# Second cross attention: turned scores ahead of scores in each slot, and two kinds of copies on VectorE instead of ScalarE

## The chip, the cores and the metric

The kernel runs on one core of a Trainium2 chip. The metric is the device time of one execution in microseconds. The core's engines work through programs of their own, each in order, and wait for each other by semaphores: TensorE (matrix products, into PSUM), VectorE, ScalarE, GpSimd, and SyncE (SP, here only a queue that starts DMAs).

## The reference

The reference is a decoder of two layers over x [16, 256, 256], each with an attention, a cross attention and experts. The change is in the cross attention of the second layer:

```python
def _L1_xattn_ref(q, k, v, mask, Wq, Wk, Wv, Wo):
    DIM, HEADS = (256, 16)
    HD = DIM // HEADS
    qh = (q @ Wq).reshape(b, s, HEADS, HD).transpose(0, 2, 1, 3)
    kh = (k @ Wk).reshape(b, s, HEADS, HD).transpose(0, 2, 1, 3)
    vh = (v @ Wv).reshape(b, s, HEADS, HD).transpose(0, 2, 1, 3)
    g = jnp.einsum('bhqd,bhkd->bhqk', qh, kh) / jnp.sqrt(jnp.float32(HD))
    g = g - mask * 1000000000.0
    A = jax.nn.softmax(g, axis=-1)
    att = jnp.einsum('bhqk,bhkd->bhqd', A, vh)
    att = att.transpose(0, 2, 1, 3).reshape(b, s, DIM)
    return att @ Wo
x = x + _L1_xattn_ref(_layernorm(x, axis=-1), ctx_1024, ctx_1024, mask_Bx1x1xS2_fk0, ...)
```

There are 16 batches of 256 queries and 256 keys, and 16 heads of 16 values.

## The kernel before, in words

The stages of the decoder run one behind the other. `l1_cross_attend` (its tiles are called x1a) gets the projected q and k as rows of heads in DRAM and v in SBUF, and does scores, softmax, the product with v, and the output projection. Sixteen heads are eight pairs (`PAIRS`), and one batch is eight **slots** h, one for each pair. `HALF` is 4, `LAG` is 6, `TPB` is 2 (256 rows are two tiles of 128).

In a slot TensorE does three things:

- `scores(b, p, h)` (L2228): four products into one of two PSUM tiles `s_ps`, of pair h of batch b, rows are queries. They serve only to find each row's maximum. It waits until VectorE's maximum of two slots before has emptied the tile. VectorE's `maximum` (L2372) reduces them, one instruction of 128x1024 values a slot, and in slots 3 and 7 `split_top` (L2378) writes the negated maxima of four pairs as a high and a low part.
- `turned_scores(b, p, h - 6)` (L2240): the same scores once more with keys as rows, six slots later: four products and, added to each by a second product (L2252), the negated maximum, which is read from `mT`. They go to the one tile `st_ps`, so they wait until ScalarE's exponentials of the slot before have emptied it. In slots 0 to 5 they are pairs 2 to 7 of the batch before. ScalarE's `exponents` (L2313) is two instructions of 128x512.
- in odd slots the **pieces**, small steps that use two PSUM banks `fill` in turn, in the order of a list (L2171). Their names are letters: M turns the maxima (half 0 in slot 5, half 1 in slot 1), P is the product of probabilities and v for two pairs, B turns that product back, O turns the normalised result, W is the output projection. A piece waits until the piece before it in its bank has been drained, and W also for O's parts.

The list: slot 1: M1, B3, P0. Slot 3: B0, O, P1. Slot 5: M0, B1, W, P2. Slot 7: B2, P3. Banks alternate along it, so P0 uses M1's bank, P1 uses B0's, W uses M0's, P2 uses B1's.

Before the change the drains are split so: ScalarE copies M (to `mT`, L2330), P (to `oT`, L2334) and O (L2338, L2340); VectorE drains B by a reciprocal and a product into `out` (L2396, L2400), and W by an addition to the resident x, followed by the row statistics. In each slot ScalarE's program has the exponentials first and then the drains of the slot in the list's order; VectorE's has the maximum, the split in slots 3 and 7, and then its drains. GpSimd copies the mask and v of a batch and makes O's low part (L2365). SP loads the rows of heads two batches ahead once the turned scores of half a batch are done (L2219).

The loops are written out for batches 0 to 3, then go over batches 4 to 15 in pairs, and batches 16 and 17 hold what is left over from 14 and 15, without scores.

Of the kernel before, what the change touches and what calls it, by code (L numbers as in the profile page):

```python
# [14 lines left out]
P = 128  # L15
BATCH = 16
SEQ = 256
# [1225 lines left out]
class Plan:  # L1243
# [21 lines left out]
    def done(self, piece, b):  # L1265

        return self.counts[piece.kind] * (b + piece.ahead) + piece.number + 1
# [579 lines left out]
PAIRS = HEADS // 2  # L1847
# [4 lines left out]
def live(b):  # L1852

    return not isinstance(b, int) or 0 <= b < BATCH
# [280 lines left out]
def l1_cross_attend(nc, sh, head_rows, wo, v, sel, mask_col, qk, top_rows):  # L2135
# [4 lines left out]
    HALF = PAIRS // 2  # L2140
    QUADS = PAIRS // 2
    LAG = 6
    with ExitStack() as ctx:
# [34 lines left out]
        def pieces_of(h):  # L2178
            return [(i,) + piece[0:3] for i, piece in enumerate(order) if piece[3] == h]
# [15 lines left out]
        with nc.Block() as block:  # L2195
# [31 lines left out]
            def _(pe):  # L2227
                def scores(b, p, h, turn):  # L2228
                    if h % HALF == 0:
                        pe.wait_ge(s_ld[p][h // HALF], 16 * LOADS * (turn + 1))  # L2230
                    if not (isinstance(b, int) and b == 0 and h < 2):
                        pe.wait_ge(s_max, PAIRS * b + h - 1)
                    for t in range(TPB):
                        for n in range(2):
                            r = slice(64 * n, 64 * n + SCORE_ROWS)
                            last = pe.matmul(s_ps[h % 2][:, n, t * SEQ:(t + 1) * SEQ], qk[p][r, 0, h, t * P:(t + 1) * P],  # L2236
                                             qk[p][r, 1, h, :], start=True, stop=True)
                    last.then_inc(s_sc, 1)
# [51 lines left out]

                def batch(b, p, turn=None):
                    for h in range(PAIRS):
                        if live(b):
                            scores(b, p, h, b // 2 if turn is None else turn)
                        if h >= LAG and live(b):
                            turned_scores(b, p, h - LAG)
                        elif h < LAG and live(b - 1):
                            turned_scores(b - 1, 1 - p, PAIRS + h - LAG)
                        for i, kind, number, ahead in pieces_of(h):
                            if live(b + ahead):  # L2300
                                piece(i, kind, number, b + ahead, p if ahead % 2 == 0 else 1 - p, b)
# [9 lines left out]
            @block.scalar  # L2311
            def _(act):
                def exponents(b, p, h):  # L2313
                    if h == 0:
                        act.wait_ge(s_vnow, b + 1)
                    act.wait_ge(s_st, PAIRS * b + h + 1)
                    c = h // 2
                    if h % 2 == 0 and not (isinstance(b, int) and b == 0 and c < 2):
                        act.wait_ge(filled["P"], QUADS * b + c - 1)
                    for j in range(TPB):  # L2320
                        last = act.activation(prob[:, c % 2, j, 2 * (h % 2):2 * (h % 2) + 2, :], st_ps[:, :, j * SEQ:(j + 1) * SEQ],  # L2321
                                              ACT.Exp, bias=mask_now[:, p, j:j + 1])
                    last.then_inc(s_exp, 1)

                def drain(i, kind, number, own):
                    bank = fill[i % 2]
                    if kind == "M":
                        act.wait_ge(filled["M"], done("M", number, own))
                        wait_past(act, s_st, PAIRS * own + HALF * (number - 1))
                        act.copy(mT[:, number, :], bank[:, 0:SEQ]).then_inc(drained["M"], 1)  # L2330
                    elif kind == "P":
                        act.wait_ge(filled["P"], done("P", number, own))
                        wait_past(act, filled["B"], QUADS * own + number - 1)
                        act.copy(oT[:, number % 2, :], bank[:, 0:SEQ]).then_inc(drained["P"], 1)  # L2334
                    elif kind == "O":
                        act.wait_ge(filled["O"], own + 1)
                        wait_past(act, s_olow, own)
                        act.copy(exact[:], bank[:])  # L2338
                        wait_past(act, filled["W"], own)
                        act.copy(outT[0][:].rearrange("p k s -> p (k s)"), bank[:]).then_inc(drained["O"], 1)  # L2340

                def batch(b, p):
                    for h in range(PAIRS):
                        if h >= LAG and live(b):
                            exponents(b, p, h - LAG)
                        elif h < LAG and live(b - 1):
                            exponents(b - 1, 1 - p, PAIRS + h - LAG)
                        for i, kind, number, ahead in pieces_of(h):
                            if live(b + ahead):
                                drain(i, kind, number, b + ahead)  # L2350

                over_two_ahead(act, batch)
# [17 lines left out]
            @block.vector  # L2370
            def _(dve):
                def maximum(b, h):  # L2372
                    dve.wait_ge(s_sc, PAIRS * b + h + 1)
                    dst = top[:, h // HALF].rearrange("p t (n i) -> p n t i", n=2)[:, :, :, h % HALF]
                    dve.tensor_reduce(dst, s_ps[h % 2][:].rearrange("p n (t s) -> p n t s", t=TPB),  # L2375
                                      AXIS.X, ALU.max).then_inc(s_max, 1)

                def split_top(b, half):  # L2378

                    done_halves = 2 * b + half  # L2380
                    dve.wait_ge(s_max, PAIRS * b + HALF * (half + 1))
                    wait_past(dve, filled["M"], done_halves - 1)
                    by_part = lambda part: top_rows[half][:, :, part::XROWS]
                    src = top[:, half]
                    dve.tensor_scalar(by_part(0), src, -1.0, None, ALU.mult).then_inc(s_neg, 1)
                    dve.wait_ge(s_neg, done_halves + 1)
                    dve.scalar_tensor_tensor(by_part(1), src, -1.0, by_part(0), ALU.mult, ALU.subtract).then_inc(s_top, 1)

                def drain(i, kind, number, own, p):
                    bank = fill[i % 2]  # L2390
                    if kind == "B":
                        n = done("B", number, own)
                        dve.wait_ge(filled["B"], n)
                        wait_past(dve, filled["O"], own - 1)
                        heads = bank[:, 0:TPB * P].rearrange("p (t g r) -> p t g r", t=TPB, r=32)
                        dve.reciprocal(rden[:, number % 2], heads[:, :, :, XROWS]).then_inc(s_rden, 1)  # L2396
                        dve.wait_ge(s_rden, n)
                        at = 4 * number * XROWS
                        dst = out[:, p, :, at:at + 4 * XROWS].rearrange("p t (g r) -> p t g r", r=XROWS)
                        dve.tensor_tensor(dst, heads[:, :, :, 0:XROWS],  # L2400
                                          rden[:, number % 2].unsqueeze(3).broadcast_to([P, TPB, 4, XROWS]), ALU.mult).then_inc(drained["B"], 1)
                    elif kind == "W":
                        dve.wait_ge(filled["W"], own + 1)
                        xb = sh.x[:, bass.ds(TPB * own, TPB), :].rearrange("p t d -> p (t d)")
                        dve.tensor_tensor(xb, xb, bank[:], ALU.add).then_inc(drained["W"], 1)
                        wait_apart(dve, drained["W"], own + 1, sh.scratch[:])
                        step = Steps(dve, s_stat, own * STATS_STEPS)
                        batch_stats(dve, step, sh, own, parts, means[:])
                        assert step.count == STATS_STEPS

                def batch(b, p):
                    for h in range(PAIRS):
                        if live(b):
                            maximum(b, h)
                            if h % HALF == HALF - 1:
                                split_top(b, h // HALF)
                        for i, kind, number, ahead in pieces_of(h):
                            if live(b + ahead):
                                drain(i, kind, number, b + ahead, p if ahead % 2 == 0 else 1 - p)

                over_two_ahead(dve, batch)
# [911 lines left out]
```

## Time and profile before

| | |
|---|---|
| median of 3 runs | 3836.72 us (3835.22 to 3844.4) |
| the profiled execution | 3845.91 us, its span 3843.2 us |
| TensorE busy over the span | 3053.0 us (79%) |
| VectorE busy | 1818.2 us (47%) |
| ScalarE busy | 1349.3 us (35%) |
| GpSimd busy | 525.5 us (14%) |
| mean granted clock of TensorE | 0.873 |

Busy time counts instructions that compute; a wait for a semaphore is idle time. The granted clock is a share of full speed; the two levels behind a mean are 0.5 and 1.00. Times in the rows further down are microseconds from the span's start, PEld is TensorE's loading of weights, and a group that is shown with x4 in a timeline is four instructions in one line, its second number the time from the first's start to the last's end. The stage in question lies at about 3043 to 3466 us.

### The profile page before, as it was taken

Reading aid. Unit: us, or ns where it says so; the run is one execution under the profiler, and the core shown is the slowest. Engines: PE = TensorE matmul, PEld = TensorE weight load, DVE = VectorE, ACT = ScalarE, POOL = GpSimd, SP = SyncE. Lnnn points to the kernel's source line nnn. Section 1 sums busy time; section 2 is a strip of 40 time slices with the busy share of each in tenths; the row PEclk is TensorE's granted clock in tenths of the full one; section 3 lists DMA queues with packets and bytes.
Section 4 is the critical chain, followed back from the end, with each engine's and each line's share of the span. In section 5 each row is a group of like instructions: output and inputs, shape, how many; then the busy total and the mean of one; then the engine's idle time right before and its main releaser. Section 6 shows DMA issues by size and latency. Waiting matters only on the chain. (4 is left out here: it accounts for less than half of the span.)

```text
span 3843.2 us, 58946 instructions
## 1 busy us (share of the span) xinstructions
PE 3053.0 (79%) x19173; PEld 2469.8 (64%) x19174; DVE 1818.2 (47%) x4053; ACT 1349.3 (35%) x3380; POOL 525.5 (14%) x488
## 2 busy tenths in 40 slices
PE   4868799999639999991499999999986777775297
PEld 3756577777526777770388888888886645554163
DVE  4553677776241222225345554545555555543423
ACT  1320244333302111113355555555553355541021
POOL 0000000000060000006122232322222000000303
PEclk9987799999759999995689999999997898885696
DMA  7000000000251111112100000000002622215264
GB/s 254 0 0 2 0 1 0 0 0 0 88 175 32 33 33 33 33 32 89 47 1 0 0 0 0 0 0 0 0 0 82 191 68 67 62 30 177 79 183 132
DMA packets 165345, 184.85 MB, mean 48 GB/s; under 512 B 22208, under 2 KB 152464, under 8 KB 163728
## 3 DMA queue, kind: packets, MB, share of 16 engines
q1 hardware_dynamic: 136464, 144.86, 12.1%
q0 software_dynamic: 9216, 25.18, 2.0%
q10 hardware_dynamic: 19584, 13.79, 1.1%
q8 instruction: 44, 0.72, 0.1%
q14 instruction: 37, 0.30, 0.0%
HBM read 115.57 MB, written 68.19 MB: 48 GB/s over the span
## 5 line engine op out<-in xcount | busy, mean ns | idle before, releaser
L1672 ACT ACTIVATE a_prob<-a_s_ps,a_ntop 128x256 f32<-128x256 f32 x512 | 240.1, 478 | 410.7 <-DVE a_ntop L1704 410.7
L1708 DVE COPY a_pT<-a_pT_ps 128x512 f32<-128x512 f32 x256 | 176.7, 690 | 354.0 <-PE a_pT_ps L1597 349.8
L1611 PE MATMUL a_o_ps<-a_v,a_pT 128*128 128x64 f32 x2048 | 270.1, 278 | 0.0
L2901 PE MATMUL e0x_up_ps<-e0w_upT,e0x_xgT 128*128 x576 | 263.6, 601 | 0.8 <-ACT e0x_xgT L2944 0.6
L1611 PEld LDWEIGHTS a_o_ps<-a_v,a_pT 128*128 128x128 f32 x2048 | 263.7, 201 | 0.0
L2919 PE MATMUL e0x_y_ps<-e0w_downT,e0x_hT 128*128 x1152 | 260.5, 379 | 1.0 <-DVE e0x_hT L2960 1.0
L2919 PEld LDWEIGHTS e0x_y_ps<-e0w_downT,e0x_hT 128*128 128x128 f32 x1152 | 218.8, 190 | 61.3 <-issue 35.2
L1702 DVE TENSOR_REDUCE a_top<-a_s_ps 128x2 f32<-128x512 f32 x256 | 175.6, 686 | 134.7 <-PE a_s_ps L1586 134.7
L2967 DVE COPY e0x_y<-e0x_y_ps 128x256 f32<-128x256 f32 x72 | 30.6, 425 | 438.7 <-PE e0x_y_ps L2919 438.7
L1799 POOL TENSOR_TENSOR a_kqT_low<-a_exact,a_kqT_high 128x512 fp32r<-128x512 f32 x128 | 163.3, 1276 | 481.9 <-ACT a_kqT_high L1659 481.9
L2375 DVE TENSOR_REDUCE x1a_top<-x1a_s_ps 128x4 f32<-128x1024 f32 x128 | 151.9, 1222 | 105.3 <-PE x1a_s_ps L2236 104.7
L2321 ACT ACTIVATE x1a_prob<-x1a_st_ps,x1a_mask_now 128x512 f32<-128x512 f32 x256 | 162.2, 684 | 104.3 <-PE x1a_st_ps L2252 104.2
L2901 PEld LDWEIGHTS e0x_up_ps<-e0w_upT,e0x_xgT 128*128 128x128 f32 x576 | 104.3, 191 | 106.4 <-issue 105.8
L2947 ACT ACTIVATE e0x_h<-e0x_up_ps 128x512 f32<-128x512 f32 x144 | 86.0, 597 | 243.8 <-PE e0x_up_ps L2901 243.8
L1597 PE MATMUL a_pT_ps<-ident,a_prob 128*128 128x128 f32 x1024 | 164.3, 286 | 0.0
L1086 ACT ACTIVATE x0b_sq<-x0b_f 128x1024 f32<-128x1024 f32 x64 | 67.9, 1061 | 261.4 <-DVE x0b_f L1158 261.4
L3004 POOL DMA_INDIRECT e0c_ya<-sorted_results,e_slots x64 | 62.2, 972 | 614.1 <-PEq L2995 594.9
L2249 PE MATMUL x1a_st_ps<-x_qk 48*128 48x256 f32 x512 | 83.7, 340 | 74.0 <-ACT x1a_prob L2321 74.0
L2944 ACT COPY e0x_xgT<-e0x_t_ps 128x256 f32<-128x256 f32 x72 | 26.8, 372 | 319.1 <-PE e0x_t_ps L2892 319.1
L1586 PE MATMUL a_s_ps<-a_kqT_high 64*128 64x256 f32 x512 | 92.0, 354 | 55.5 <-ACT a_prob L1672 54.4
L1597 PEld LDWEIGHTS a_pT_ps<-ident,a_prob 128*128 128x128 f32 x1024 | 129.1, 150 | 6.9 <-issue 2.6
L1041 PE MATMUL x_bank<-x0b_b_sb,x0b_gT 128*128 128x256 f32 x512 | 118.6, 385 | 7.3 <-issue 3.7
(544 smaller groups left out, 7630.6 us busy)
## 6 DMA issues: line engine op xcount, KB each, us to landing
x_qk<-head_rows SPq DMA_DIRECT2D x384, 64.0 KB
head_rows<-x1p_rows_out SPq DMA_DIRECT2D x32, 512.0 KB, 3.5
e1w_ew<-in_L_ffn_expert_w_dram SPq DMA_DIRECT2D x8, 2048.0 KB, 17.9
sorted_tokens<-zeros SPq DMA_DIRECT2D x12, 1024.0 KB, 21.2
e1x_xg<-sorted_tokens SPq DMA_DIRECT2D x96, 128.0 KB, 2.2
sorted_results<-e1x_y ACTq DMA_DIRECT2D x96, 128.0 KB, 2.3
e0x_xg<-sorted_tokens SPq DMA_DIRECT2D x72, 128.0 KB, 2.0
sorted_results<-e0x_y SPq DMA_DIRECT2D x72, 128.0 KB, 1.7
```

What stands on the lines that cost most here:

```text
L1041: pe.matmul(o[:, t * DIM:(t + 1) * DIM], gT[:, h, t * P:(t + 1) * P], b_sb[:, h, :], start=h == 0, stop=False)
L1586: last[n] = pe.matmul(s_ps[n][:, t, :], kqT[x][r, c, 1, t * P:(t + 1) * P], kqT[y][r, c, 0, :], start=i == 0, stop=i == len(HIGH_LOW) - 1)
L1597: last = pe.transpose(pT_ps[h % 2][:, j, t * P:(t + 1) * P], prob[:, h % 4, t, j * P:(j + 1) * P], sh.ident[:])
L1611: last = pe.matmul(o_ps[q % 2][:, at:at + dh], pT[:, h % 4, j, t * P:(t + 1) * P], v[:, j, h * dh:(h + 1) * dh], start=j == 0, stop=j == T ...
L1672: ins = act.activation(prob[:, h % 4, t, :], src, ACT.Exp, bias=ntop[:, h % 4, t:t + 1], accum_out=den[:, t, h:h + 1])
L1702: dve.tensor_reduce(top[:, h % 4, :], s_ps[s][:], AXIS.X, ALU.max).then_inc(s_max, 1)
L1708: dve.tensor_copy(pT[:, h % 4], pT_ps[h % 2][:]).then_inc(s_pT, 1)
L1799: pool.tensor_tensor(low, src, top_part, ALU.subtract).then_inc(drained[p.kind], 1)
L2321: last = act.activation(prob[:, c % 2, j, 2 * (h % 2):2 * (h % 2) + 2, :], st_ps[:, :, j * SEQ:(j + 1) * SEQ], ACT.Exp, bias=mask_now[:, p ...
L2375: dve.tensor_reduce(dst, s_ps[h % 2][:].rearrange("p n (t s) -> p n t s", t=TPB), AXIS.X, ALU.max).then_inc(s_max, 1)
L2901: last = pe.matmul(up_ps[half][:], xgT[:, p, k, :], upT[:, bass.ds(e, 1), k, half * 512:(half + 1) * 512].rearrange("p a d -> p (a d)"), s ...
L2919: last = pe.matmul(y_ps[p][:, 0:DIM], hT[:, p, c, :], downT[:, bass.ds(e, 1), c, :].rearrange("p a d -> p (a d)"), start=c == 0, stop=c == ...
```

## The change

It has two parts. In TensorE's program the turned scores of a slot come before its scores. And the drains of M and P, two and four copies of 128x256 a batch, go from ScalarE's program to VectorE's, where they take their place in the list's order behind the maximum (and split) of their slot. The waits of the copies are the same, and so are all sizes, buffers and the list of pieces.

```diff
                 def batch(b, p, turn=None):
                     for h in range(PAIRS):
-                        if live(b):
-                            scores(b, p, h, b // 2 if turn is None else turn)
                         if h >= LAG and live(b):
                             turned_scores(b, p, h - LAG)
                         elif h < LAG and live(b - 1):
                             turned_scores(b - 1, 1 - p, PAIRS + h - LAG)
+                        if live(b):
+                            scores(b, p, h, b // 2 if turn is None else turn)
                         for i, kind, number, ahead in pieces_of(h):
...
                 def drain(i, kind, number, own):
                     bank = fill[i % 2]
-                    if kind == "M":
-                        act.wait_ge(filled["M"], done("M", number, own))
-                        wait_past(act, s_st, PAIRS * own + HALF * (number - 1))
-                        act.copy(mT[:, number, :], bank[:, 0:SEQ]).then_inc(drained["M"], 1)
-                    elif kind == "P":
-                        act.wait_ge(filled["P"], done("P", number, own))
-                        wait_past(act, filled["B"], QUADS * own + number - 1)
-                        act.copy(oT[:, number % 2, :], bank[:, 0:SEQ]).then_inc(drained["P"], 1)
-                    elif kind == "O":
+                    if kind == "O":
...
                 def drain(i, kind, number, own, p):
                     bank = fill[i % 2]
-                    if kind == "B":
+                    if kind == "M":
+                        dve.wait_ge(filled["M"], done("M", number, own))
+                        wait_past(dve, s_st, PAIRS * own + HALF * (number - 1))
+                        dve.tensor_copy(mT[:, number, :], bank[:, 0:SEQ]).then_inc(drained["M"], 1)
+                    elif kind == "P":
+                        dve.wait_ge(filled["P"], done("P", number, own))
+                        wait_past(dve, filled["B"], QUADS * own + number - 1)
+                        dve.tensor_copy(oT[:, number % 2, :], bank[:, 0:SEQ]).then_inc(drained["P"], 1)
+                    elif kind == "B":
```

## Rows read from the trace of the kernel before

**Rows 1.** Busy time by stretch: engines' busy us, then TensorE's granted clock, DMA.
```profile
3043.30:3466.00 422.70, 303.15 (x3008) 208.88 (x3008) 223.98 (x448) 210.92 (x385) 31.44 (x44) 0.84 0.20 59
3426.00:3447.00 21.00, 14.78 (x140) 8.93 (x133) 5.99 (x18) 11.64 (x21) 1.27 (x1) 0.74 0.00 0
```

**Rows 2.** Waits in the stage: who waited for whom, us, times, longest.
```profile
ACT x1a_prob L2321 <- PE x1a_st_ps L2252: 104.2, 127, 1.3
...
PE x1a_st_ps L2249 <- ACT x1a_prob L2321: 74.0, 65, 2.3
...
PE x1a_fill L2270 <- ACT x1a_mT L2330: 16.6, 16, 1.0
...
PE x1a_fill L68 <- ACT x1a_mT L2330: 14.5, 14, 1.0
...
PE x1a_fill L2270 <- DVE x1a_out L2400: 3.1, 12, 0.6
```

**Rows 3.** Timeline of TensorE, slots 0 to 3 (start, length, what, idle before).
```profile
3331.97 0.50 PE L2236 MATMUL x1a_s_ps<-x_qk 50*128 50x256 f32 x4
3332.31 0.29 PE L2249 MATMUL x1a_st_ps<-x_qk 48*128 48x256 f32 x2
...
3332.79 0.40 PE L2236 MATMUL x1a_s_ps<-x_qk 50*128 50x256 f32 x4
3334.40 0.39 PE L2249 MATMUL x1a_st_ps<-x_qk 48*128 48x256 f32 x2 [1.21 <-ACT x1a_prob L2321]
...
3335.07 0.44 PE L2263 MATMUL x1a_fill<-ident,x_top_rows 128*128 128x128 f32 x2
...
3336.76 1.07 PE L2270 MATMUL x1a_fill<-x1a_prob,x1a_v_now 128*32 128x256 f32 x16 [1.04 <-ACT x1a_mT L2330]
...
3340.11 0.38 PE L2249 MATMUL x1a_st_ps<-x_qk 48*128 48x256 f32 x2 [1.13 <-ACT x1a_prob L2321]
...
3341.84 1.07 PE L2270 MATMUL x1a_fill<-x1a_prob,x1a_v_now 128*32 128x256 f32 x16 [0.19 <-DVE x1a_out L2400]
```

**Rows 4.** Timeline of all engines, slots 0 and 1 of another batch.
```profile
3206.14 0.50 PE L2236 MATMUL x1a_s_ps<-x_qk 50*128 50x256 f32 x4
...
3206.68 2.36 DVE L2375 TENSOR_REDUCE x1a_top<-x1a_s_ps 128x4 f32<-128x1024 f32 x2 [0.54 <-PE x1a_s_ps L2236]
...
3210.43 0.37 ACT L2330 CAST x1a_mT<-x1a_fill 128x256 fp32r<-128x256 f32 x1
...
3210.86 1.79 PE L2270 MATMUL x1a_fill<-x1a_prob,x1a_v_now 128*32 128x256 f32 x16 [1.04 <-ACT x1a_mT L2330]
```

**Rows 5.** Timeline, slot 5: turned scores, first product of W, end of statistics.
```profile
3220.68 0.39 PE L2249 MATMUL x1a_st_ps<-x_qk 48*128 48x256 f32 x2 [1.13 <-ACT x1a_prob L2321]
...
3223.06 0.39 PE L68 MATMUL x1a_fill<-x_wo_high,x1a_outT_high 128*128 128x256 f32 x1 [1.04 <-ACT x1a_mT L2330]
...
3226.80 0.17 DVE L261 TENSOR_SCALAR x_stats<-x1a_means 128x4 f32 x1 [0.15 <-DVE x1a_means L258]
```

**Rows 6.** Timeline of VectorE, slots 2 and 3: maxima, split, drain of B0.
```profile
3213.42 2.48 DVE L2375 TENSOR_REDUCE x1a_top<-x1a_s_ps 128x4 f32<-128x1024 f32 x2 [3.03 <-PE x1a_s_ps L2236]
3216.04 0.18 DVE L2385 TENSOR_SCALAR x_top_rows<-x1a_top 128x16 fp32r<-128x16 f32 x1
3216.26 0.19 DVE L2387 SCALAR_TENSOR_TENSOR x_top_rows<-x1a_top,x_top_rows 128x16 fp32r<-128x16 f32 x1
3216.75 0.21 DVE L2396 RECIPROCAL x1a_rden<-x1a_fill 128x8 f32<-128x8 f32 x1 [0.30 <-PE x1a_fill L2276]
3216.99 0.29 DVE L2400 TENSOR_TENSOR x1a_out<-x1a_fill,x1a_rden 128x128 f32<-128x128 f32 x1
```

**Rows 7.** Groups by line: busy us, mean ns of one, idle before.
```profile
L2967 DVE COPY e0x_y<-e0x_y_ps 128x256 f32<-128x256 f32 x72 | 30.6, 425 | 438.7 <-PE e0x_y_ps L2919 438.7
```

**Rows 8.** Busy time by stretch: behind slot 1's stall, and over slots 2, 3.
```profile
3210.50:3214.00 3.50, 3.15 (x28) 2.02 (x30) 0.58 (x1) 0.68 (x3) 0.00 (x0) 0.58 0.41 124
...
3338.60:3343.70 5.10, 3.78 (x52) 2.62 (x50) 3.25 (x7) 3.77 (x7) 0.50 (x1) 1.00 0.31 94
```

## The prediction

> **What bounds the kernel now.** The page comes first: over the whole span TensorE is the busiest engine, but that is a mean over six stages, and the change touches one of them, the attention of the second cross attention (tiles x1a). So I went on with the stretch that this stage fills, 3043.3 to 3466.0 us: of its 422.7 us TensorE is busy 303, VectorE 224, ScalarE 211 [rows 1]. No engine is full; what sets the pace is a chain that goes from one engine to another. The table of waits names its links: TensorE waits 74.0 us for exponentials before turned scores and 16.6 + 14.5 us for the copy of the turned maxima, mT, but only 3.1 us for VectorE's normalised out [rows 2].
>
> Then I followed one batch in the timeline. It has eight slots h; write S(h) for its scores, T(h) for the turned scores that stand in slot h, X(h) for the two exponentials that follow. Pieces stand only in odd slots. In slots 0 and 1 the trace has S(0) at 3331.97, T(0) at 3332.31, S(1) at 3332.79; then TensorE idles 1.21 us until X(0) has emptied the turned bank; T(1) at 3334.40, piece M1 at 3335.07, B3, an idle 1.04 us, and P0 at 3336.76 [rows 3]. So S of an even slot lies on the path, and S of the odd slot hides in the wait for X. X(1) runs while the pieces do. The idle before P0 is M1's copy: it stands on ScalarE behind X(1) [rows 4]. Slot 5 has the same stall before the first product of W, 2.38 us behind T(5) (3220.68 to 3223.06) [rows 5]. Slot 3 has almost none: T(3) at 3340.11, P1 at 3341.84 after 0.19 us [rows 3], since there the maxima and their split are done about when B0 lands.
>
> **The change part by part.** *S and T change places.* In even slots S leaves the path and goes under X(h). It takes 0.34 us there (3331.97 to 3332.31) [rows 3]; the group that stands first bears a longer start, whichever it is, so I take 0.22 as saved; the ends are 0.1 and 0.34. In odd slots S now comes behind T, where nothing hides it unless the pieces wait anyway. In slot 7 they don't wait and it costs the same 0.22: that pair comes out even. In slots 1, 3 and 5 they do, as follows.
>
> *VectorE gets the odd maximum later.* Until now S(odd)'s data were there before T(odd), and VectorE took both maxima in one go, 2.36 us for two [rows 4], 1.2 for one. Now, counted from T(odd)'s start, S starts at +0.48 (as T(0) to S(1), 3332.31 to 3332.79 [rows 3]), its maximum 0.54 later (3206.14 to 3206.68 [rows 4]), at +1.02, and it ends at +2.24. VectorE works through its program in order, and its pieces stand behind that maximum.
>
> *M1 and M0 on VectorE.* The copy can start at about +2.27. The trace has no VectorE copy of this very tile; its copy of 128x256 out of PSUM takes 425 ns [rows 7], ScalarE's of mT takes 0.37 us [rows 4]. The source and shape are those of the first, so I take 0.43, with ends of 0.37 and, should the change of type cost a second pass, 0.85. TensorE is released 0.06 after (3210.43 + 0.37 to 3210.86 [rows 4]): at +2.75. It was at +2.36 (3334.40 to 3336.76 [rows 3]). So 0.39 less the 0.22 of the even S: 0.17 us for slot 1, and as much for slot 5. Here the Trainium skill (VectorE: DVE Perf Modes, the cycle table in the section on the TRN2 errata) gives a VectorE copy from PSUM 120 cycles and one for each element at 0.96 GHz, thus 0.39 us, an estimate, and ScalarE's 0.36: by it the sum would be lower by 0.03 us a copy, 1 us in all. The measured 425 ns decides.
>
> *B0 in slot 3.* P1 fills the bank that B0 filled, so it waits for B0's normalisation on VectorE, and that now stands behind the late maximum and the split of the maxima. The split starts 0.14 us after the maxima (3213.42 + 2.48 to 3216.04) and ends 0.41 later; reciprocal and product take 0.53 (3216.75 to 3217.28) [rows 6], the release 0.06. So P1 starts at 2.24 + 0.14 + 0.41 + 0.53 + 0.06 = +3.38; it was at +1.73. That is 1.65 less 0.22 = 1.4 us for each batch, the largest term, and it comes from no operation that the diff names. Its ends: 1.1 if VectorE's instructions overlap, 1.7 if the even S saves nothing.
>
> *P's copies on VectorE.* P is filled when the pieces end, and its reader B is two slots on. The copy stands ahead of the next even maximum, but that one's data come 1.02 us after T(even), and P's copy is over about 0.5 us after it. So S's new place hides it; with S still first it would be late by nothing or 0.1. In slot 5 it stands behind W's sum and statistics, which end 3.9 us after W's first product (3223.06 to 3226.97 [rows 5]); then the maximum of slot 6 starts some 0.7 us late, which TensorE would feel only two slots later. ScalarE, rid of both copies, gains nothing on the path: its exponentials wait for TensorE's turned scores 127 times, nearly each pair of them, 104.2 us [rows 2], so the copies did not hold them up.
>
> *Waits that move.* M's copy waits for older turned scores, P's for an older B; both are met a slot or more earlier. Queued behind them on VectorE are maxima, and behind these TensorE's S two slots on. SP's loads wait for T of slots 1 and 5 and are used some seven slots later. GpSimd waits for P's matmuls, not for its copy, and for O, whose copies stay on ScalarE. All this costs nothing as long as that slack of slots is there; without it each late maximum would cost its 1.2 us.
>
> *Sum.* 0.17 + 0.17 + 1.4 = 1.74 us a batch. Slots that hold both scores and pieces of the batch before are in batches 1 to 15: 15 x 1.74 = 26 us. The filling adds some 2 (T(0) waits for M0's copy behind the sixth maximum; slot 5 of batch 1 waits for B1 as slot 3 does for B0); in batch 16 no maximum stands ahead of M1's copy, and 0.8 us comes back. Together 27.
>
> *The clock.* In the 3.5 us that begin in the idle before P0 the granted clock is 0.58, while it is 1.00 over slots 2 and 3 of another batch, where TensorE hardly idles [rows 8]. So it falls from 2.4 to 1.2 GHz behind a wait, in slot 1 of nearly every batch. What one fall costs: 3.5 us x 0.42 lost x the 3.15 of 3.50 us that TensorE was busy = 1.3 us. The change puts 1.6 us of idle before P1. In batch 16, which has no scores and so idles more, the clock is 0.74 over 21 us [rows 1]. Whether slot 3 will fall as slot 1 does I can only bound: nothing, or 15 x 1.3 = 20 us. I take about half, 9 us, since slot 5, with a wait like slot 1's, ran at 1.00 in some batches.
>
> So 27 + 9 = 36 us. The profiled execution took 3845.9 us (span 3843.2); the median of the runs is 3836.7, 9.2 us less. On the median 3836.7 + 36 = about 3873.
>
> **Rivals.** *One: the copy goes ahead (faster).* If VectorE is idle when M lands, it empties M at once: M ends 1.1 us behind T's start (3334.40 to 3335.07 + 0.44), copy and release take 0.49, so the product starts at +1.6 instead of +2.36, 0.8 us earlier, twice a batch: 24 us less, 3813. That 31.1 us of TensorE's waits are for this copy [rows 2] speaks for it. It decides if the odd maximum is over before M has landed, thus if S(odd) starts over half a microsecond before T(odd); the new order puts it 0.48 behind. Batch 16 is the only place where it holds.
>
> *Two: nothing to be measured.* The work between the two waits, T, S, M, B, is longer by 0.22 us; if that keeps the clock at 2.4 GHz in slot 1, 12 x 1.3 = 15 us return, and if slot 3 doesn't fall either the sum is 27 - 15 = 12: 3849. Against it: the idle before P0 grows.
>
> *Three: the clock falls in slot 3 of every batch and in slot 5 too.* Ten more falls in slot 5 are 13 us, slot 3 gives 20: 3836.7 + 27 + 33 = 3897. For it is batch 16, against it that falls now come once or twice a batch, not three times.
>
> **How the numbers follow.** Forecast 0.60, at 3873 (alone 3858 to 3886: slot 3's term 1.1 to 1.7, falls none to all). Rival three 0.20, rival two 0.13, rival one 0.07. To leave out no more than 2 in 10 the range goes from 3850 to 3900. What a measurement of this kernel can tell from no change is about 0.3%, 11.5 us: below 3825 is faster, above 3848 slower. Slower: 0.60 + 0.20, and a little of rival two, whose time lies at the bound: 0.81. Same 0.12, faster 0.07.
>
> **What would show it.** In slot 3 B0's reciprocal starts behind the split, and TensorE idles some 1.6 us before P1; its 3.1 us of waits for out become about 25. The waits for mT remain, with VectorE as releaser, and grow from 31 to some 36. The stage becomes 450 to 465 us, the others stay. Even maxima start within 0.3 us of their data, except in slot 6. The prediction is wrong if P1 starts within 2 us of T(3), or if the stage's granted clock rises above its 0.84 [rows 1].

## The result, and the profile after

The changed kernel takes 3878.9 us (median of 4 runs, 3871.5 to 3883.9) where the kernel before took 3837.9 beside it: ratio 1.0109, with a 95% interval of 1.0086 to 1.0133. It is slower by 1.1%, 41 us between the two medians. The forecast was 3873 with a range of 3850 to 3900.

The profiled execution has a span of 3874.2 us, 31 more than before. By stretches, the stage of the change grew by more than that: from 421.7 us to 465.7, counted from the start of the first scores to the start of the last statistics (3043.3 to 3465.0 and 3029.6 to 3495.3; the stretch of [rows 1] ends 1 us later). The difference lies in an earlier stage that the change doesn't touch, the second layer's self attention: it took 992.0 us in the profile of before and 978.1 in this one, with granted clocks of 0.94 and 0.95. So the stage, not the span, is what is compared below. Busy time by stretch, columns as in [rows 1]; of the kernel after first the self attention, the whole stage, twelve steady batches from the M0 of one batch to another's, and two batches that ran at the full clock from end to end, each from M1 to M1:

```profile
1903.90:2882.00 978.10, 888.43 (x7361) 829.71 (x7362) 509.48 (x1096) 538.65 (x1710) 269.57 (x211) 0.95 0.00 0
...
3029.60:3495.30 465.70, 330.57 (x3008) 226.06 (x3008) 259.23 (x543) 179.64 (x289) 31.48 (x44) 0.76 0.19 54
...
3121.15:3451.93 330.78, 237.45 (x2259) 163.49 (x2257) 194.28 (x408) 133.63 (x217) 24.83 (x36) 0.80 0.20 56
...
3109.10:3132.99 23.89, 15.73 (x190) 11.04 (x188) 16.01 (x34) 11.10 (x19) 2.08 (x3) 1.00 0.25 69
3214.89:3239.18 24.29, 15.73 (x191) 11.05 (x189) 16.20 (x34) 11.10 (x19) 2.08 (x3) 1.00 0.24 66
```

The same of before, the self attention, twelve steady batches and a batch at the full clock, from M0 to M0:

```profile
1903.00:2895.00 992.00, 904.37 (x7359) 844.40 (x7360) 509.33 (x1096) 538.98 (x1710) 269.50 (x211) 0.94 0.00 0
...
3122.10:3421.26 299.16, 219.03 (x2259) 151.19 (x2257) 168.01 (x336) 157.04 (x288) 24.77 (x36) 0.87 0.21 62
...
3323.19:3345.87 22.68, 15.74 (x191) 11.04 (x189) 13.94 (x28) 13.02 (x24) 2.06 (x3) 1.00 0.23 71
```

Two things are to be seen. A batch at the full clock went from 22.68 us to 23.89 in the quickest case and to 24.29 in a usual one: 1.2 to 1.6 us more of waiting. The quickest is the first batch that ran at the full clock; the half of a batch with slots 1 to 4 (M1 to M0) took 12.05 us there and 12.31 to 12.42 in the five others that had the full clock, against 10.80 before. And the granted clock over the steady batches fell from 0.87 to 0.80. The two levels being 1.00 and 0.5, the time at 1.2 GHz is twice the missing share: (1 - 0.87) x 2 x 299 = 78 us before and (1 - 0.80) x 2 x 331 = 132 us after. Twelve batches are 31.6 us longer; some 12 x 1.6 = 19 of it are waits, and 12 are left for the clock. Of the 44.0 us of the stage some 13 lie ahead of the steady batches, where the pipeline fills: that part went from 78.8 to 91.5 us, its clock from 0.78 to 0.65.

The time at 1.2 GHz does not come in more pieces. Read in steps of 0.2 us, the clock is low 14 times over the steady batches before and 12 times after; what grew is the length. Before, four of these last 10 us and none is longer. After, seven last 10 us or more, three of them over 20. Here are one of 10 us of before and one of 20 us of after, each a little shorter than the whole:

```profile
3184.00:3193.80 9.80, 8.86 (x72) 5.93 (x64) 3.94 (x7) 4.36 (x8) 1.27 (x1) 0.50 0.21 66
...
3295.80:3315.80 20.00, 15.98 (x106) 11.31 (x110) 8.20 (x18) 6.14 (x10) 1.27 (x1) 0.50 0.23 64
```

The first begins behind the wait of slot 1 and is over before slot 5. The second begins in the wait of slot 1 too, and lasts over the waits of slots 3 and 5. Four of the twelve begin in the wait of slot 3 or just behind it, where none does before.

Where the waits are, one batch at the full clock shows. Timeline of the kernel after, slots 1, 3 and 5 (VectorE's lines are L2367 maximum, L2377 and L2379 split, L2386 M's copy, L2390 P's copy, L2396 and L2400 B):

```profile
3108.19 0.39 PE L2249 MATMUL x1a_st_ps<-x_qk 48*128 48x256 f32 x2 [1.13 <-ACT x1a_prob L2321]
...
3109.21 1.23 DVE L2367 TENSOR_REDUCE x1a_top<-x1a_s_ps 128x4 f32<-128x1024 f32 x1 [0.81 <-PE x1a_s_ps L2236]
...
3110.35 0.41 DVE L2386 CAST x1a_mT<-x1a_fill 128x256 fp32r<-128x256 f32 x1
...
3110.82 1.07 PE L2270 MATMUL x1a_fill<-x1a_prob,x1a_v_now 128*32 128x256 f32 x16 [1.07 <-DVE x1a_mT L2386]
...
3111.96 0.42 DVE L2390 COPY x1a_oT<-x1a_fill 128x256 f32<-128x256 f32 x1 [0.75 <-PE x1a_fill L2270]
...
3112.84 1.23 DVE L2367 TENSOR_REDUCE x1a_top<-x1a_s_ps 128x4 f32<-128x1024 f32 x1 [0.46 <-PE x1a_s_ps L2236]
3113.93 0.39 PE L2249 MATMUL x1a_st_ps<-x_qk 48*128 48x256 f32 x2 [1.13 <-ACT x1a_prob L2321]
...
3114.97 1.23 DVE L2367 TENSOR_REDUCE x1a_top<-x1a_s_ps 128x4 f32<-128x1024 f32 x1 [0.90 <-PE x1a_s_ps L2236]
...
3116.23 0.18 DVE L2377 TENSOR_SCALAR x_top_rows<-x1a_top 128x16 fp32r<-128x16 f32 x1
...
3116.55 0.20 DVE L2396 RECIPROCAL x1a_rden<-x1a_fill 128x8 f32<-128x8 f32 x1
...
3117.12 1.07 PE L2270 MATMUL x1a_fill<-x1a_prob,x1a_v_now 128*32 128x256 f32 x16 [1.40 <-DVE x1a_out L2400]
...
3120.23 0.39 PE L2249 MATMUL x1a_st_ps<-x_qk 48*128 48x256 f32 x2 [1.12 <-ACT x1a_prob L2321]
...
3122.88 0.39 PE L68 MATMUL x1a_fill<-x_wo_high,x1a_outT_high 128*128 128x256 f32 x1 [1.07 <-DVE x1a_mT L2386]
```

P0 starts 2.63 us behind T(1) (2.36 before), P1 3.19 behind T(3) (1.73 before), W 2.65 behind T(5) (2.38 before). In slot 3 the idle before P1 is 1.40 us where it was 0.19 [rows 3], and VectorE's order is to be read off its four rows: maximum, split, then B0's reciprocal. From T(1) to T(3) it is 5.74 us against 5.71, from T(3) to T(5) 6.30 against 5.08: all of the 1.21 us is between T(3) and T(5), with the wait for P1 in it. In the batch of 24.29 us the same wait is longer by 0.21 us:

```profile
3219.81 0.39 PE L2249 MATMUL x1a_st_ps<-x_qk 48*128 48x256 f32 x2 [1.20 <-ACT x1a_prob L2321]
...
3220.83 1.23 DVE L2367 TENSOR_REDUCE x1a_top<-x1a_s_ps 128x4 f32<-128x1024 f32 x1 [0.95 <-PE x1a_s_ps L2236]
...
3222.30 0.18 DVE L2377 TENSOR_SCALAR x_top_rows<-x1a_top 128x16 fp32r<-128x16 f32 x1 [0.24 <-DVE x1a_top L2367]
...
3223.20 1.07 PE L2270 MATMUL x1a_fill<-x1a_prob,x1a_v_now 128*32 128x256 f32 x16 [1.61 <-DVE x1a_out L2400]
```

P1 is 3.39 us behind T(3) here: the split starts 0.24 us after the maximum where it was 0.03 in the first batch. Of the seven batches that had the full clock from T(3) to P1, one has 3.19, one 3.29, four 3.39 and one 3.65. The table of waits points to the same place; what answers to [rows 2]:

```profile
PE x1a_st_ps L2249 <- ACT x1a_prob L2321: 74.7, 65, 2.3
...
PE x1a_fill L2270 <- DVE x1a_out L2400: 21.7, 16, 1.9
...
PE x1a_fill L2270 <- DVE x1a_mT L2386: 16.3, 16, 1.1
...
PE x1a_fill L68 <- DVE x1a_mT L2386: 10.9, 14, 1.1
```

### The profile page after: what moved, and what is told of

The parts are those of the page before. It is cut to its first block and busy times, and to the rows that moved or that the text cites. A ratio compares the mean times of both kernels' runs of the same rounds, so it can differ in the third digit from the quotient of the medians.

```text
span 3874.2 us, 58886 instructions
## 1 busy us (share of the span) xinstructions
PE 3069.5 (79%) x19173; PEld 2473.3 (64%) x19174; DVE 1853.4 (48%) x4149; ACT 1317.7 (34%) x3284; POOL 526.1 (14%) x488
## 5 line engine op out<-in xcount | busy, mean ns | idle before, releaser
L2367 DVE TENSOR_REDUCE x1a_top<-x1a_s_ps 128x4 f32<-128x1024 f32 x128 | 156.4, 1225 | 107.4 <-PE x1a_s_ps L2236 107.1
L2249 PE MATMUL x1a_st_ps<-x_qk 48*128 48x256 f32 x512 | 96.4, 387 | 76.5 <-ACT x1a_prob L2321 74.7
L2249 PEld LDWEIGHTS x1a_st_ps<-x_qk 48*128 48x128 f32 x512 | 58.9, 227 | 128.5 <-ACT x1a_prob L2321 94.6
```

Of the source, the lines that this page charges most:

```text
L2249: pe.matmul(st_ps[:, n, at], qk[p][r, 1, h, j * P:(j + 1) * P], qk[p][r, 0, h, :], start=True, stop=False)
```

## The experiments

The theory after the result: (a) the odd maximum comes after M and B0 in time but ahead of them in VectorE's program, so they wait for it, and this is the cost of the new order, not of the copies; (b) the new idle of slot 3 gives TensorE more time at the lower clock. Rivals: the copies cost because they are on VectorE; the scores behind the turned scores cost by themselves; the clock is chance. The stage's length is compared as well as the time, since the rest of the kernel varies by more than 10 us from one profile to the next. The profile is that of one run, and that run is not always a usual one: in e1, e3 and e6 it was the slowest of its group (e1 21 us above the median), in e9 the fastest (14 us below) and in e10 15 us below the median. The groups of runs were on chips whose kernel before took 3838 to 3870 us; the ratios are each to the kernel before on the same chip.

### e1: the order alone

```diff
-                        if live(b):
-                            scores(b, p, h, ...)
                         if h >= LAG and live(b):
                             turned_scores(b, p, h - LAG)
                         elif h < LAG and live(b - 1):
                             turned_scores(b - 1, 1 - p, PAIRS + h - LAG)
+                        if live(b):
+                            scores(b, p, h, ...)
```

> The turned scores ahead of the scores, the copies left on ScalarE. Theory (the new place of the odd scores makes the odd maximum late and B0 of slot 3 stands behind it): M is still copied behind the exponentials, so P0 starts 2.36 us behind T(1) as before; slot 3 has P1 at about 3.2 us behind T(3) instead of 1.73. That is +1.2 us a batch in slot 3, less 0.24 in slots 1 and 5 each: +0.7 us x 15 = +11 us, and with more time at the lower clock +10 to +25 in all. Rival (the two copies on VectorE are what costs): no change, or 7 us faster by the even scores.

Ratio 1.0057 (1.0035 to 1.0078), stage 454.9 us, 33 more than before: the order by itself makes the kernel slower. Slots 1 and 3 of a batch, timeline of TensorE:

```profile
3137.40 0.38 PE L2249 MATMUL x1a_st_ps<-x_qk 48*128 48x256 f32 x2 [1.12 <-ACT x1a_prob L2321]
3139.76 1.94 PE L2270 MATMUL x1a_fill<-x1a_prob,x1a_v_now 128*32 128x256 f32 x16 [0.80 <-ACT x1a_mT L2330]
3144.21 0.39 PE L2249 MATMUL x1a_st_ps<-x_qk 48*128 48x256 f32 x2 [0.97 <-ACT x1a_prob L2321]
...
3147.41 1.93 PE L2270 MATMUL x1a_fill<-x1a_prob,x1a_v_now 128*32 128x256 f32 x16 [1.40 <-DVE x1a_out L2400]
```

P0 is 2.36 us behind T(1), as expected, and P1 3.20 behind T(3), as in the changed kernel. The stage grew by more than the 10 to 25 us expected; the granted clock over its steady batches was 0.77. The whole kernel grew by 0.57%, 22 us; its stage is read from the profile of the slowest of ten runs, and one profile is one draw of the clock, as e8 shows.

### e2: the copies alone

The old order stays, and the drains of M and P move as in the change:

```diff
-                        act.copy(mT[:, number, :], bank[:, 0:SEQ]).then_inc(drained["M"], 1)
...
-                        act.copy(oT[:, number % 2, :], bank[:, 0:SEQ]).then_inc(drained["P"], 1)
...
+                        dve.tensor_copy(mT[:, number, :], bank[:, 0:SEQ]).then_inc(drained["M"], 1)
...
+                        dve.tensor_copy(oT[:, number % 2, :], bank[:, 0:SEQ]).then_inc(drained["P"], 1)
```

> The copies of M and P on VectorE, the scores left ahead of the turned scores. Theory: the odd maximum is over before M lands, so VectorE empties M at once: P0 and W start about 1.6 us behind T instead of 2.36, 0.76 us x 2 x 15 = 23 us faster; P's copy delays the even maximum by some 0.1 us, which nobody waits for; slot 3 as before. With less idle before P0 the clock may give another 0 to 20 us: 3795 to 3815. Rival (the copies on VectorE cost, since its queue is longer): 5 to 25 us slower than before.

Ratio 0.9942 (0.9916 to 0.9969), stage 401.6 us, 20 less than before. The copies do not cost, they gain, and the rival falls. Slot 1:

```profile
3194.89 0.39 PE L2249 MATMUL x1a_st_ps<-x_qk 48*128 48x256 f32 x2 [1.21 <-ACT x1a_prob L2321]
...
3195.57 0.44 PE L2263 MATMUL x1a_fill<-ident,x_top_rows 128*128 128x128 f32 x2
...
3196.14 0.42 DVE L2386 CAST x1a_mT<-x1a_fill 128x256 fp32r<-128x256 f32 x1 [0.63 <-PE x1a_fill L2263]
...
3196.62 1.07 PE L2270 MATMUL x1a_fill<-x1a_prob,x1a_v_now 128*32 128x256 f32 x16 [0.40 <-DVE x1a_mT L2386]
```

VectorE sits idle 0.63 us until M lands and empties it at once; P0 is 1.73 us behind T(1) instead of 2.36. This is rival one of the prediction; what it needs is that the odd maximum is out of the way when M lands. By the ratio it is 22 us faster on this chip, at the lower edge of the 22 to 42 expected; the medians (3844.0 beside 3855.9) differ by 12 only, so the size is less sure than the sign.

### e9: M's copies alone on VectorE, old order

```diff
-                        act.copy(mT[:, number, :], bank[:, 0:SEQ]).then_inc(drained["M"], 1)
...
+                        dve.tensor_copy(mT[:, number, :], bank[:, 0:SEQ]).then_inc(drained["M"], 1)
```

> The old order, only the copies of M on VectorE, P's left on ScalarE. Theory (the gain of the copies is M alone, since no exponential waits for P's copy): the stage takes 395 to 408 us, as with both copies (401.6), and the fastest pair of slots 4 to 1 and 0 to 5 stay at 10.1 and 11.1 us. Rival (P's copies held up ScalarE's exponentials, so freeing ScalarE of them is part of the gain): the stage takes more than 410 us.

Ratio 0.9913 (0.9881 to 0.9946), stage 384.5 us, shorter than the theory had expected, and the rival is refuted: freeing ScalarE of P's copies is no part of the gain. From M1 to M0 the quickest case took 10.05 us, and 10.07 with both copies moved (e2); but the usual ones at the full clock took 10.05 to 10.16 here and 10.22 to 10.32 in e2, so P's copies on VectorE cost a little, some 0.15 us a batch. The 17 us between the two stages, 401.6 and 384.5, are mostly something else: they came with granted clocks of 0.84 and 0.89, and e9's profile is that of its fastest run. Whether P's copies have a part in the clock is open, and the intervals of the ratios overlap.

### e3: changed kernel, B0 drained ahead of the third maximum

```diff
                 def batch(b, p):
                     for h in range(PAIRS):
+                        early = [x for x in pieces_of(h) if h == 3 and x[1] == 'B']
+                        for i, kind, number, ahead in early:
+                            if live(b + ahead):
+                                drain(i, kind, number, b + ahead, ...)
                         if live(b):
                             maximum(b, h)
...
```

> The changed kernel, but in slot 3 VectorE drains B0 ahead of the third maximum. Theory (B0 in VectorE's queue is the largest term): P1 starts about 1.9 us behind T(3) instead of 3.19, so 1.2 to 1.3 us x 15 = 19 us faster than the changed kernel, plus some of the 24 us that the clock took: 3835 to 3860. Rival (the cost is the clock or TensorE's order, whoever is first in VectorE's queue): within 8 us of the changed kernel's 3879.

Ratio 1.0000 (0.9983 to 1.0016), stage 428.5 us, 37 less than the changed kernel. One instruction pair in another place of VectorE's program, with all copies and TensorE's order as changed, takes the loss away. TensorE in slot 3:

```profile
3192.99 0.39 PE L2249 MATMUL x1a_st_ps<-x_qk 48*128 48x256 f32 x2 [1.02 <-ACT x1a_prob L2321]
3194.18 0.60 PE L2281 MATMUL x1a_fill<-ident,x1a_out 128*128 128x128 f32 x4
3194.97 1.07 PE L2270 MATMUL x1a_fill<-x1a_prob,x1a_v_now 128*32 128x256 f32 x16 [0.19 <-DVE x1a_out L2400]
```

P1 is 1.98 us behind T(3), and the idle before it is 0.19 us again.

### e4: M drained ahead of the maximum as well

```diff
-                        early = [x for x in pieces_of(h) if h == 3 and x[1] == 'B']
+                        early = [x for x in pieces_of(h) if (h == 3 and x[1] == 'B') or x[1] == 'M']
```

> The changed kernel with VectorE draining M in slots 1 and 5 and B0 in slot 3 ahead of the slot's maximum. Theory (the place in VectorE's queue is what costs): P0 and W start about 1.8 us behind T instead of 2.63, 0.8 us x 2 x 15 = 25 us less than with B0 alone ahead (stage 428.5), and a better clock: stage 385 to 405, ratio to before about 0.99 to 0.997. Rival (scores behind the turned scores cost by themselves): the stage stays above 415.

Ratio 0.9935 (0.9911 to 0.9960), stage 395.9 us. P0 stands 1.86 us behind T(1) (3249.52 and 3251.38 in its timeline, an idle of 0.30 us). So TensorE's new order costs nothing that can be measured once the late maximum doesn't stand ahead of what TensorE waits for; the rival of the order is out. It isn't better than the old order with the copies moved (e2) either.

```profile
3249.52 0.39 PE L2249 MATMUL x1a_st_ps<-x_qk 48*128 48x256 f32 x2 [1.13 <-ACT x1a_prob L2321]
3251.38 1.07 PE L2270 MATMUL x1a_fill<-x1a_prob,x1a_v_now 128*32 128x256 f32 x16 [0.30 <-DVE x1a_mT L2386]
```

### e5, e10 and e6: the clock

To tell the clock from the waits, needless products are put into TensorE's idle, behind a wait that is already met, into a scores tile whose maximum has been taken. They change nothing that is computed.

```diff
+                def filler(b, p, h, times):
+                    if times:
+                        pe.wait_ge(s_max, PAIRS * b + h)
+                    for _ in range(times):
+                        for t in range(TPB):
+                            for n in range(2):
+                                r = slice(64 * n, 64 * n + SCORE_ROWS)
+                                pe.matmul(s_ps[(h - 1) % 2][:, n, t * SEQ:(t + 1) * SEQ], qk[p][r, 0, h, t * P:(t + 1) * P],
+                                          qk[p][r, 1, h, :], start=True, stop=True)
...
+                            if at == 2 and live(b) and not (isinstance(b, int) and b == 0):
+                                filler(b, p, h, {1: 4, 3: 5, 5: 4}.get(h, 0))
```

e5 is the changed kernel with this, e10 the changed kernel with `{3: 5}` alone, e6 the kernel before with `{1: 4, 5: 4}`.

> The changed kernel with needless products in TensorE's idle waits of slots 1, 3 and 5 (16, 20 and 16 products into a scores tile whose maximum is taken; 0.9 to 1.1 us each at the full clock, into waits of 1.07 and 1.40 us). Nothing of the result uses them. Theory (half of the loss is TensorE's clock, which falls behind idle waits): the stage's granted clock rises from 0.76 to above 0.9 and it is 20 to 45 us shorter although it does more. Rival (the clock falls anyway, or the fillers delay the pieces at the lower clock): the stage is 0 to 30 us longer.

> The changed kernel with the 20 needless products in TensorE's wait of slot 3 only. Theory (the new idle of slot 3 is what brings the clock down more often than before): over the steady batches the time at the lower clock goes back from some 11.5 to 16 us a batch to about the 6.7 of the kernel before, and the stage takes 430 to 445 us. Rival (the falls come from the waits of slots 1 and 5, which were there before, or from all alike): less than half of it goes, the stage stays above 450.

> The kernel before with 16 needless products in TensorE's idle wait of slots 1 and 5 each (into a scores tile whose maximum is taken; nothing of the result uses them), as the changed kernel with fillers has them. Theory (waits on VectorE's queue and the clock each cost about half): the granted clock rises above 0.92, and the stage takes 380 to 390 us, some 20 us less than the 401.4 of the changed kernel with fillers, which is 1.33 us x 15, the longer waits alone. Rival (the longer waits cost nearly nothing by themselves and the clock is all of the loss): the two with fillers are within 6 us of each other, 395 to 407.

Twelve steady batches of each, in the order e5, e10, e6:

```profile
3128.14:3428.03 299.89, 240.40 (x2883) 177.70 (x2881) 193.84 (x408) 133.22 (x217) 24.86 (x36) 0.97 0.22 62
```

```profile
3143.23:3454.42 311.19, 228.01 (x2498) 162.90 (x2497) 193.67 (x408) 133.11 (x217) 24.77 (x36) 0.91 0.21 60
```

```profile
3128.80:3405.39 276.59, 218.86 (x2643) 159.52 (x2641) 167.18 (x336) 156.00 (x288) 24.76 (x36) 0.98 0.23 67
```

*e5.* 624 more products, and 30.9 us less (330.8 to 299.9), with the clock at 0.97 instead of 0.80. The whole stage:

```profile
3047.20:3470.00 422.80, 329.33 (x3788) 241.58 (x3788) 258.45 (x543) 179.12 (x289) 31.53 (x44) 0.92 0.21 59
```

It took 422.8 us where it took 465.7, 42.9 less, inside the 20 to 45 expected. (The 401.4 us that the expectation of e6 gives for e5 count from its first filler at 3068.6, not from its first scores at 3047.2.) In runs: ratio 1.0014 (0.9995 to 1.0032), against 1.0109 for the changed kernel without them. The fillers do not change the waits: P1 is 3.3 to 3.4 us behind T(3) in most batches, as in the changed kernel, and TensorE still idles before it until VectorE's out is there:

```profile
3225.71 1.07 PE L2270 MATMUL x1a_fill<-x1a_prob,x1a_v_now 128*32 128x256 f32 x16 [0.23 <-DVE x1a_out L2412]
```

So what they give back is the clock.

*e10.* Fillers in slot 3 alone: clock 0.91, time at 1.2 GHz (1 - 0.91) x 2 x 311 = 56 us, less than the 78 of the kernel before; stage 433.3 us, inside the 430 to 445 expected. The clock still falls behind slots 1 and 5, eleven times in the steady batches, but ten of these falls are short and only one lasts 20 us. So what the idle of slot 3 did was to keep the clock low once it had fallen, as far as one profile of each can show. Fillers in slots 1 and 5 of the changed kernel without slot 3 were not run; e6 shows that they too lift the clock in the kernel before. The ratio, 1.0068 (1.0045 to 1.0092), is a step of 16 us away from 1.0109, half of the stage's 32; the profiled run was 15 us quicker than the median of its ten.

*e6.* The kernel before with fillers: stage 394.5 us, ratio 0.9935 (0.9910 to 0.9960). The expectation was 380 to 390, and 20 us below e5; the stage was 4.5 over it, and 28.3 below e5's 422.8. Over the twelve steady batches the two differ by 299.9 - 276.6 = 23.3 us. A batch at the full clock takes 24.3 us in e5 and 22.7 here, so 12 x 1.6 = 19 of it are the longer waits, and some 4 are the clock. So the rival (the clock is everything) falls too.

From before to e6 the time at 1.2 GHz went from 78 to 11 us and the batches from 299.2 to 276.6: 0.34 us for each. From the changed kernel to e5 it went from 132 to 18 us, for 30.9 us: 0.27. With these prices the 54 us more at 1.2 GHz are 15 to 18 us, where the waits leave 12 over: the same size, and no closer, since the clock is read to two digits and the waits are not the same in every batch.

### e8: the changed kernel again

> The changed kernel as it is, beside the others of this group, so that they are compared on one chip. Both theories expect a ratio to before of 1.009 to 1.013 and a stage of 455 to 475 us.

Ratio 1.0120 (1.0085 to 1.0156). The profile's stage took 474.1 us with the clock at 0.73, 8 us more than in the first: the draw of the clock is worth that much between two executions of one program. Over its steady batches the clock is low 16 times, nine of them for 10 us or more.

```profile
3035.30:3509.40 474.10, 339.63 (x3008) 232.23 (x3008) 259.43 (x543) 179.66 (x289) 31.38 (x44) 0.73 0.18 53
```

### e7 and e11: versions that beat both

The old order with both copies (e7) or M's alone (e11) on VectorE, and fillers in the other idle, the wait for the exponentials of even slots, into the bank that the slot's first piece overwrites:

```diff
+                def bank_filler(b, p, h, times):
...
+                    for _ in range(times):
+                        pe.matmul(fill[i % 2][:, 0:SEQ], qk[p][0:SCORE_ROWS, 0, h, 0:P], qk[p][0:SCORE_ROWS, 1, h, :], start=True, stop=True)
...
+                        if h % 2 and live(b) and not (isinstance(b, int) and b < 2):
+                            bank_filler(b, p, h, 9)
```

> The old order with the copies of M and P on VectorE (stage 401.6 us), and nine needless products of 50x128 by 256 in TensorE's wait for the exponentials of the even slot, ahead of the odd turned scores, into the bank that the slot's first piece overwrites. They take about 1.0 of the 1.2 us at the full clock. Theory (idle waits bring the clock down and it costs 0.27 us for each us at 1.2 GHz): the clock goes from 0.84 to above 0.93 and the stage to 365 to 385, ratio to before 0.98 to 0.99. Rival (the clock stays, or the fillers run over): the stage takes 400 to 420.

> The old order, only M's copies on VectorE (stage 384.5 us, clock 0.89), with the nine needless products in the wait for the exponentials of even slots. Theory (the two gains add, and what fillers can give is the time still spent at the lower clock, 30 us in the steady batches and more in the filling ones, at 0.3 us each): the stage takes 370 to 380 us, ratio to before 0.985 to 0.989. Rival (fillers in this wait run over by as much as they give): 382 to 390 us.

e7: ratio 0.9883 (0.9857 to 0.9910), stage 379.9 us. e11: ratio 0.9873 (0.9856 to 0.9889), stage 371.8 us. Both stages lie in what the theory expected; between the two the intervals of the ratios don't decide. Twelve steady batches of e7 (3114.76 to 3371.86), also at a clock of 1.00, took 257.1 us, 2 more than those of e11, which are P's copies again. The steady batches of e11, all at the full clock:

```profile
3139.40:3394.40 255.00, 239.82 (x2690) 183.31 (x2688) 175.08 (x360) 149.67 (x264) 24.84 (x36) 1.00 0.26 73
```

Twelve batches in 255.0 us instead of 299.2. Without needless work, e9 has the shortest stage and the lowest ratio that was run, but the intervals of e2, e4 and e9 overlap.

## Why the prediction was right, point by point

*Sign and size.* Forecast 36 us, measured 41 in the medians and 44.0 in the stage. The stage was to take 450 to 465 us and took 465.7, and 474.1 when it was profiled again.

*VectorE's queue.* Right, down to the times: the odd maximum starts 1.02 us behind T(1) as worked out, and P1 in most batches at +3.29 to +3.39, worked out +3.38. The sum was 1.74 us a batch; measured 1.21 in the quickest batch and 1.6 in the others, thus 24 us over 15 batches instead of 26. Slot 3 was to give 1.4 and gave 1.2 to 1.5. It is 1.2 in the batch of the timeline, since there the split starts 0.03 us after the maximum and the reciprocal 0.32 after the split; this is near the low end of 1.1, with VectorE's instructions overlapping. Slots 1 and 5 were to give 0.17 each and gave 0.03 to 0.12 and nothing: P0 is at +2.63 instead of +2.75. The term that was mis-sized is the hand-over between VectorE's instructions, which I took as 0.03 us after the end; M's copy starts at 3110.35, 0.09 us before the maximum's row ends, and lasts 0.41 us, not 0.43. The cycle table of the Trainium skill (VectorE: DVE Perf Modes, TRN2 errata) gave 0.39, a little low.

*The clock.* The direction was right, and the size, 9 us, was half of what the runs leave: 44.0 - 24 - 1 = 19 over the stage (the 1 for filling and draining is the forecast's own and was not measured). The forecast took the falls of slot 3 as short ones beside those of slot 1, 1.3 us each, in half of the batches. What came was about as many falls as before (12 instead of 14 in the steady batches), but long ones: the clock stayed low over the wait of slot 3 for up to 20 us, where it had come back after at most 10. So that step named the right place and the wrong mechanism, and the 9 us were a halfway guess between its bounds. Part of the miss lies ahead of the steady batches, where the clock went from 0.78 to 0.65. The Trainium skill (TensorE: Matmul & The Clock Gate, Terms) puts the penalty at the throttled time x (1 - K/N), half of it; the runs here show 0.27 to 0.34. A reason that fits, though no run tests it alone, is that part of TensorE's work at 1.2 GHz fills idle time that is there anyway: the idle before W is 1.07 us at the full clock and 0.61 at the low one.

*Copies and ScalarE.* P's copies cost nothing on the path: in the timeline P0's copy ends 0.46 us before the next maximum could start. In the old order they cost some 0.15 us a batch (e7 beside e11), where the prediction had said nothing or 0.1 us late. ScalarE gained nothing from being rid of them (e9). In slot 6 the maximum was 0.3 us late, not 0.7.

*Marks.* The waits for out came to 21.7 us (said 25). The waits for mT were to grow from 31 to 36 and fell to 27: at the lower clock TensorE's own pieces take up the idle before W (0.61 us for 1.07). That mark was wrong.

*Rivals.* Rival one could not come about with M's copy queued behind the late maximum, and e2 and e4 show that its mechanism is real: 20 and 26 us in the stage. Rival two, the clock giving back, had the wrong sign. Rival three, a fall in slots 3 and 5 of every batch, put 33 us on the clock: 14 above the 19 that came, where the forecast was 10 below.

## What to carry to other kernels

Before an instruction that a partner waits for is moved to another engine, ask what stands ahead of it in that engine's program and when that can run: here 1.2 us of a maximum that nobody was waiting for stood ahead of a copy that TensorE was idle for, and putting B0's drain one place forward took back the whole 1.1%, clock and all. Two edits made together can have opposite signs and need not add up: the order alone gave +0.6%, the copies alone -0.6%, and both together +1.1%, since the late maximum also took away what the copies gain. So price and test them apart and together. And price an added idle of TensorE twice, once as time and once as the clock that it may lose: in this stage the waits were some 24 us and the clock some 19.

## What the runs showed of the hardware that was not expected

Needless products in idle waits make the kernel faster: e11 has 432 more in its twelve batches than e9, and they take 255.0 us with the clock at 1.00, where e9's take 266.7 at 0.95 (3127.47 to 3394.19). In e5 and e6 each microsecond less at 1.2 GHz was worth 0.27 and 0.34 us. No idle of TensorE in the steady batches before was longer than 1.2 us, and yet its clock was at 1.2 GHz for 78 of 299 us; with a wait of some 1.4 us before P1 (16.5 us over twelve batches) in place of 0.2 the longest low stretches went from 10 to 20 us. The same program spends different times at 1.2 GHz from one execution to the next (0.76 and 0.73 over this stage, 465.7 and 474.1 us), and the self attention, untouched in all, took 978.1 and 992.0 us in two profiles. VectorE's row for a copy begins 0.09 us before the row of the maximum ahead of it ends, where the two read different tiles.
